# Attention scores of the last stage: the low pass cut to 64 rows per column half, with key parts swapped and query's low part doubled

## What is computed

```
for l in range(L):
    q = (x @ Wq[l] + bq[l]).reshape(N, H, D)
    k = (x @ Wk[l] + bk[l]).reshape(N, H, D)
    v = (x @ Wv[l] + bv[l]).reshape(N, H, D)
    a = (q[dst] * k[src]).sum(-1) * scale
    ...
    alpha = e / (denom[dst] + 1e-16)
    agg = segment_sum(alpha[:, :, None] * v[src], dst).reshape(N, C)
    x = agg + (x @ Ws[l] + bs[l]) + enc
```

## Time and profile before

| | |
|---|---|
| runs, median (lowest to highest) | 1126.06 us (1126.03 to 1126.74) |
| the profiled execution: its time | 1126.59 us |
| its span, first to last instruction | 1124.8 us |
| mean granted TensorE clock | 0.987 |
| PE busy, PEld busy | 1070.4 us, 991.7 us |
| DVE, POOL, ACT busy | 772.2 us, 681.3 us, 574.0 us |

### The profile page before, as it was taken

One profiled execution on the slowest core, in us unless ns is written; L12 is line 12 of the kernel. 1 busy time (PEld: TensorE's weight loads), 2 busy tenths in 40 slices (PEclk: granted clock), 3 DMA queues, 4 the chain that ended last, 5 costly groups with the idle time before them and its releaser, 6 DMA issues.

```text
span 1124.8 us, 20713 instructions
## 1 busy us (share of the span) xinstructions
PE 1070.4 (95%) x6808; PEld 991.7 (88%) x6808; DVE 772.2 (69%) x1530; ACT 574.0 (51%) x1027; POOL 681.3 (61%) x930
## 2 busy tenths in 40 slices
PE   7999898899999999999999999999999999999797
PEld 7899897699988999889998899987999889998795
DVE  7899755766667566675666756676778867777634
ACT  7999655445421454214542135424676636676340
POOL 3232467755587555875557755499656866478671
PEclk9999999899999999999999999999999999999899
DMA  5100001422012120121201212122101201021101
GB/s 128 30 1 1 7 20 65 144 71 85 1 48 85 59 85 1 48 85 59 85 1 48 85 48 76 60 89 76 66 1 41 73 1 47 1 76 39 38 1 46
DMA packets 40963, 56.92 MB, mean 51 GB/s; under 512 B 14312, under 2 KB 14812, under 8 KB 40735
## 3 DMA queue, kind: packets, MB, share of 16 engines
q1 hardware_dynamic: 40600, 55.37, 15.3%
q10 hardware_dynamic: 260, 0.21, 0.1%
HBM read 51.44 MB, written 4.12 MB: 49 GB/s over the span
## 4 chain that ended last, share of the span: by engine, by line
PE 81%; DVE 6%; ACT 4%; POOL 4%; issue 3%; DMA 0%; DVEq 0%; POOLq 0%; PEldq 0%; ACTq 0%
PE ps L340 44%; PE ps L1747 8%; PE ps L362 8%; PE ps L774 5%; PE ps L2080 3%; PE ps L2007 3%; PE ps L2381 2%; ACT away L732 1%; PE ps L1721 1%; PE ps L1226 1%; PE ps L2044 1%; PE ps L1239 1%; POOL w_lo L380 1%; DVE stats L384 1%; ACT prob L436 1%
## 5 line engine op out<-in xcount | busy, mean ns | idle before, releaser
L380 POOL TENSOR_TENSOR w_lo<-w_raw,w_hi 128x512 fp32r<-128x512 f32 x152 | 203.5, 1339 | 12.7
L340 PE MATMUL ps<-yt_hi,w_hi 128*128 128x314 f32 (+2 forms) x640 | 201.7, 315 | 2.1 <-DVE yt_lo L2215 1.6
L340 PE MATMUL ps<-yt_hi,w_lo 128*128 128x314 f32 (+2 forms) x640 | 197.6, 309 | 0.0
L340 PE MATMUL ps<-yt_lo,w_hi 128*128 128x314 f32 (+2 forms) x640 | 197.1, 308 | 0.0
L459 POOL TENSOR_SCALAR prob<-prob,rinv 125x628 f32<-125x628 f32 x160 | 126.3, 791 | 103.9 <-DVE rinv L444 85.3
L403 ACT ACTIVATE pt_hi<-ps 125x625 fp32r<-125x625 f32 x160 | 109.2, 694 | 102.8 <-PE ps L362 101.7
L377 POOL TENSOR_SCALAR w_hi<-w_raw 128x512 fp32r<-128x512 f32 x152 | 97.9, 644 | 96.6 <-DMA w_raw<-L_gnn_wo 31.7
L340 PEld LDWEIGHTS ps<-yt_hi,w_hi 128*128 128x128 f32 x640 | 121.7, 190 | 5.1 <-issue 2.8
L340 PEld LDWEIGHTS ps<-yt_hi,w_lo 128*128 128x128 f32 x640 | 121.6, 190 | 0.0
L340 PEld LDWEIGHTS ps<-yt_lo,w_hi 128*128 128x128 f32 x640 | 121.5, 190 | 0.1
L774 PE MATMUL ps<-oh_s,oh_d 125*125 125x314 bf16 x800 | 111.9, 301 | 10.0 <-DVE oh_s L639 6.7
(11 more groups left out here) (317 smaller groups left out, 2798.5 us busy)
## 6 DMA issues: line engine op xcount, KB each, us to landing
w_raw<-L_gnn_m_w SPq DMA_DIRECT2D x8, 1024.0 KB, 5.4
w_raw<-L_gnn_W SPq DMA_DIRECT2D x6, 1024.0 KB, 5.4
w_raw<-L_gnn_wv SPq DMA_DIRECT2D x4, 1024.0 KB, 6.4
w_raw<-L_gnn_wq SPq DMA_DIRECT2D x4, 1024.0 KB, 5.5
w_raw<-L_gnn_wk SPq DMA_DIRECT2D x4, 1024.0 KB, 7.3
w_raw<-L_gnn_wo SPq DMA_DIRECT2D x4, 1024.0 KB, 6.2
w_raw<-L_gnn_Wv SPq DMA_DIRECT2D x2, 1024.0 KB, 5.4
w_raw<-L_gnn_Wq SPq DMA_DIRECT2D x2, 1024.0 KB, 5.4
```

The source lines that it names most:

```text
L340: ins = pe.matmul(out_ap, lhs(i, kk), rhs(j, kk), start=kk == 0 and n == 0, stop=kk == count - 1 and n == 2)
L380: pool.tensor_tensor(w[slot][1][:, kk, 0:cols], w_raw[slot][:, kk, 0:cols], w[slot][0][:, kk, 0:cols].bitcast(FP32), ALU.subtract).then_in ...
```

## The change

The three products of a score tile stay the same, and so does the number of matmuls. In the second column half the two parts of key change places: high where low was. Query's low part is doubled, as its high part is, so that each half of the columns finds it in the rows that face key's high part. The low pass then takes 64 rows of `ql` and `kd` alone: rows 0 to 63 for one column half and rows 64 to 127 for the other (64-row slices which, from the operands, occupy different halves of the array's rows). The loops change places: first both halves of the high pass, then both of the low pass. Key's parts are written by two instructions of 314 columns in place of one of 628, on ACT and on DVE; ACT gets 8 copies more per layer (`dl:`); the four fills with zeros go, and so does their semaphore; new semaphores tell of the first halves and of the copies.

```diff
 LAYER_ACT (start of the table)
-hi:q0e hi:q0o du:q0e du:q0o hi:k0e hi:k0o exp:s0_0 exp:s0_1 hi:q1e hi:q1o hi:t0_0 exp:s0_2 exp:s0_3 hi:t0_1
+hi:q0e hi:q0o du:q0e du:q0o hi:k0e hi:k0o dl:q0e exp:s0_0 exp:s0_1 dl:q0o hi:q1e hi:q1o hi:t0_0 exp:s0_2
...
 middle_dve
-                    if not more and name == f_order[0]:
-                        for even, odd in ql:
-                            dve.memset(even[64:128, :].bitcast(FP32), 0.0).then_inc(s_qpad, 1)
-                            dve.memset(odd[0:64, :].bitcast(FP32), 0.0).then_inc(s_qpad, 1)
...
 layers_dve
+                    dve.wait_ge(s_kh, it * len(k_hi_order) + k_hi_order.index(name) + 1)
+                    for half in range(2):
+                        cols, h0 = slice(H2 * half, H2 * half + H2), 64 - p0 if half else p0
+                        dve.scalar_tensor_tensor(out=kd[c % 2][odd][64 - h0:128 - h0, cols],
+                                                 in0=ps[s][p0:p1, 512 * half:512 * half + H2],
+                                                 scalar=bk3[p0:p1, b:b + 1], op0=ALU.add, op1=ALU.subtract,
+                                                 in1=kd[c % 2][odd][h0:h0 + 64, cols].bitcast(FP32)
+                                                 ).then_inc(done if half else s_kl, 1)
...
 layers_act
+                    for half in range(2):
+                        h0 = 64 - p0 if half else p0
+                        act_hi(act, jobs, name[:2], 0, kd[c % 2][odd][h0:h0 + 64, H2 * half:H2 * half + H2],
+                               ps[s][p0:p1, 512 * half:512 * half + H2], s_hi3 if half else s_kh, bk3[p0:p1, b:b + 1])
+                elif kind == "dl":
+                    c, odd = int(name[1]), int(name[2] == "o")
+                    if odd:
+                        jobs.wait_drained(act, f"q{c}")
+                    else:
+                        act.wait_ge(s_even, it * len(even_order) + even_order.index(name) + 1)
+                    lower = ql[c % 2][odd]
+                    act.activation(lower[64 - 64 * odd:128 - 64 * odd, :], lower[64 * odd:64 * odd + 64, :].bitcast(FP32),
+                                   ACT.Copy).then_inc(s_dl, 1)
...
 layers_pe
-                        pe.wait_ge(s_qpad, 4)
...
+                        pe.wait_ge(s_dl, it * len(low_order) + low_order.index(f"q{c}{'eo'[odd]}") + 1)
+                        pe.wait_ge(s_kl, it * len(k_lo_order) + k_lo_order.index(f"k{c}{'eo'[odd]}") + 1)
                     s = jobs.acquire(pe, name)
-                    for half in range(2):
-                        for n, part in enumerate((qd, ql)):
-                            ins = pe.matmul(ps[s][0:R, 512 * half:512 * half + H2], part[c % 2][odd][:, t_slice(t)],
-                                            kd[c % 2][odd][:, H2 * half:H2 * half + H2], start=n == 0, stop=n == 1)
+                    for n in range(2):
+                        for half in range(2):
+                            h0 = 64 - 64 * odd if half else 64 * odd
+                            part, rows_in = (ql, slice(h0, h0 + 64)) if n else (qd, slice(0, 128))
+                            ins = pe.matmul(ps[s][0:R, 512 * half:512 * half + H2],
+                                            part[c % 2][odd][rows_in, t_slice(t)],
+                                            kd[c % 2][odd][rows_in, H2 * half:H2 * half + H2], start=n == 0, stop=n == 1)
```

## The result

| | before | changed |
|---|---|---|
| median (lowest to highest), 4 runs each on the same chip | 1126.40 us (1126.03 to 1127.21) | 1146.50 us (1145.30 to 1147.46) |
| profiled execution: time, span | 1126.59, 1124.8 us | 1146.43, 1144.6 us |
| mean granted TensorE clock | 0.987 | 0.985 |

The ratio is 1.0174, with a 95% interval of 1.0159 to 1.0189. The forecast was 1148 us, from 1138 to 1157.

A forecast was written before the change was run, and what follows sets the result against it. The prediction took PE to bound the kernel, with 81% of the chain. Score tiles on the chain 18.9, those beside it 1 and layer starts 2.3 made 22.2 us on 1126.6: 1148.8, taken as 1148, range 1138 to 1157.

The forecast's parts named there:

- The turn: PE going 128 to 64 rows and back in each score tile: 0.235 in, 0.09 plus 0.105 us out.
- a change of number format: Doubt whether part of the turn's gaps in the entry stage belonged to their own format; with soaked-up waits, 1138 us.
- x: Delay from a tile's first low pass to its second: bounded by 0, 0.105 and 0.145 us, taken as 0.05.
- What is felt of PE's part: Longer score tiles felt in the layers: 18.9 us on the chain plus 1 us beside it.
- the 64 tiles on the chain: Some 64 of 80 score tiles lie on the chain, each 0.295 us longer: 18.9 us, felt in full.
- The 16 tiles beside the chain: Score tiles beside other engines' work: 4.7 us more at most, counted as 1.
- ACT and DVE: Added copies and halved key parts, felt only at each layer's start: first scores 1.15 us late, 2.3 us for two layers.
- rival 2: ACT becomes a second bound or PE's clock falls more often: up to 12 us on top, 1157 to 1165; chance 0.06.
- the copies farther on: Later `dl:` copies on ACT: counted as nothing, at most 0.7 us for each of six.
- The sum: Whole kernel: 18.9 + 1 + 2.3 = 22.2 us more, giving 1148 us.

The follow-up runs named there:

- e3: The kernel before with only the loops changed to high, high, low, low in each tile, 128 rows throughout: 1126.98 us, ratio 1.0004.
- e2: The kernel before with only the low passes cut to 64 rows, both on the same 64: 1159.09 us, ratio 1.0304.
- e5: The changed kernel with its loops as before (high, low, high, low), so PE turns four times a tile: 1198.71 us, ratio 1.0668.
- e6: The changed kernel with two neighbouring score tiles of a head sharing a turn, 5 places a layer: 1143.99 us, ratio 1.0155.
- e10: The kernel before with low passes cut to 64 rows in the two array halves, ACT and DVE work unchanged: 1139.90 us, ratio 1.0124.
- e4: The changed kernel with the copy `dl:q0e` put ahead of the first keys on ACT: 1142.81 us, ratio 1.0149.
- e9: The changed kernel with `dl:q0e` moved ahead of the keys and `dl:q0o` behind the high parts of `q1`: 1140.88 us, ratio 1.0129.
- e1: The changed kernel with the low pass on all 128 rows, low by low computed on top: 1134.90 us, ratio 1.0069.
- e12: The kernel before plus the 8 copies per layer and their waits, 128 rows, fills gone: 1129.73 us, ratio 1.0032.
- e11: The kernel before with key's parts written as two instructions each, in their old rows: 1126.84 us, ratio 1.0003.
- e8: The changed kernel with 128 rows in the low pass and both early copies, `dl:q0e` and `dl:q0o`, moved: 1133.31 us, ratio 1.0061.
- e13: e9 with DVE starting on a key's first half as soon as ACT has written it: 1140.41 us, ratio 1.0124.

## Why the prediction held, and which terms were off

**The turn (right).** 0.235 in, 0.09 and an unhidden load of 0.105 out, read from three other places, are what the tiles show; the 0.235 is the median of all 80 in the changed kernel's trace. The doubt that those places owed it to a change of number format is settled: here all passes have the same one. The Trainium skill's rule in TensorEngine Tiling (Array Packing), Tiling Modes, that a change of mode drains the engine, agrees with the 0.235 us, where 0.145 and hidden loads stand without a change. e3 (no turn, no loss), e2 (turns without the pair, 0.14 more a tile) and e5 (twice the turns, 0.38 for each) bear it out; e6 doesn't, since its gain is no more than what the clock gave it.

**x (mis-sized).** 0.05 was the middle between nothing and one load after the other. The tile at 826 us shows both loads and both passes side by side. Over 64 tiles that is 3.2 us too much; without it the turns come to 64 x 0.245 + 1 = 16.7.

**What is felt of PE's part (mis-sized, a little).** e10 shows 13.7 timed, 12.6 in the trace of the layers. The step that failed is that for the 64 tiles on the chain "no other path can undo that". Two things stand between 16.7 and 12.6 in the profile: the stretch at half clock that the kernel before had at 908 us is missing in e10 (1.5 us), and PE waits 2.3 us less for POOL. That leaves 12.9, but the agreement is in part luck. Counted by PE's own time, all 80 tiles are longer, 80 x 0.245 = 19.6; less 1.5 of clock and 2.7 of all waits (DVE's among them) that is 15.4, and 2.8 stay unexplained. So a share of a chain, times a cost per piece, was 3 to 4 us too high in 17; the waits that surround the chain's pieces soak up some of it. The 16 tiles beside the chain can't be told apart from it.

**ACT and DVE (mis-sized, the largest error).** 2.3 us were forecast, 6.4 measured (20.1 less e10's 13.7). The mechanism and its place were right, the copy `dl:q0e` behind two keys: 1.33 late and not 1.15, twice, 2.7 us. The rest, 3.7 us, was not in the sum. By the traces it is the clock. At the end of the layers the changed kernel is 7.1 us behind e10 (1073.1 and 1066.0), which has the same tiles: 0.95 by its first score (800.89 and 799.94; ACT began 0.36 early), 1.3 at the second layer's start (1.73 us from the last projection to the scores, 0.40 in e10), and 4.6 in the three stretches at half clock, of which e10 has none. That is 6.9 of 7.1; one wait has grown by 1.2 (`pt_lo`), and the one for POOL has shrunk by as much. e4 and e9, which have no such stretch in their layers, are 3.7 and 5.6 us faster than the changed kernel though the start gains just 1.0. It is what rival 2 named (PE's clock falls more often), at well under half its price.

The same work is also felt in another way when PE is fast. With 128 rows (e1) it costs 7.2 us in the layers, and that with no half clock in them, where the kernel before lost 1.5: the starts 2.7, the place behind `dl:q0o` 1.6 (2.2 less 0.6), 1.1 more waiting for POOL. The other 3.3 no single wait shows. That the copies farther on count for nothing held for the changed kernel and would have been wrong for that one. The parts alone (e12 3.5, e11 0.6, e10 13.7: 17.8) fall 2.3 short of the whole; the changed kernel has more stretches at half clock than any of them, and e11 left out the change of rows, which lengthens each pair by 0.13.

**The sum.** 3.2 us too much for x and 3.0 too much for what is felt (16.7 less 13.7) stand against 4.1 too little for ACT, DVE and the clock (6.4 less 2.3): 22.2 forecast, 20.1 measured. The total is closer than its terms because these cancel, and that is luck.

**What stays open:** why the stretches at half clock lie where they do. PE idles 1.4 us at the start of each layer in the changed kernel, in e1 and in e6 alike; only the changed kernel has one 2 us behind it, in both layers. That the idle start is what brings them (e4 fits it) is not shown. In e1 and e8 two lie in the entry stage, at another place than before, in a program that is the same there. No run changed this by itself.

## What to carry to other kernels

Cutting matmuls to half the rows to run two at once pays only by the block: here a turn in and out cost 0.39 us of PE and the overlap gave back 0.145 a pair, so at least three pairs must share a turn, and in this order of work at most two stand together. Count the turns in the schedule before counting the matmuls saved. A copy added to an engine that works in order costs by where it stands, not by its length: put it behind whatever frees a slot or feeds another engine, and look for the next late operand once it is moved (in e4 DVE's key part took 0.8 of the 1.3 us). And when a sum comes out right, check its terms apart.

## What the runs showed of the hardware that was not expected

- Two 64-row passes in the two halves of the array overlap fully, loads included: 0.41 us for two of 405 ns, 2 to 5 ns apart, right behind the turn; on the same 64 rows they took 0.55 (e2).
- Some kernels that turn were granted less of PE's clock, by unequal amounts from run to run of the same program: 0.988 to 0.972 in e2, with times from 1150.4 to 1165.2 us; 0.975 to 0.962 in e5; 0.984 to 0.991 in e3 and the kernel before. Turning alone doesn't do it: e10, e9 and e13 turn twice a tile and have 0.987 to 0.993. Why e2, with as many turns, loses more is not explained.
- Two instructions of 314 columns on a key's parts take 1.06 us on ACT and 1.11 on DVE when the second uses other rows than the first, against 0.93 and 0.99 when both use the same (e11). Each is as long as before, 0.52 on ACT; in e11 the second starts before the first has ended, in the changed kernel it doesn't.
